# First stage of a graph kernel: its bulk loads issued by SyncE between the rounds instead of by ScalarE at the start

## The reference

```python
x0, x1 = _lin_irreps(x0, x1, W_up0, W_up1)          # of the layer-normed x, 1250 nodes x 512
h = edge_feats                                       # 40000 edges x 8
for W in (W_mlp1, W_mlp2, W_mlp3):
    h = SILU_2MOM * jax.nn.silu(h @ W / jnp.sqrt(jnp.float32(W.shape[0])))
tpw = h @ W_mlp4 / jnp.sqrt(jnp.float32(W_mlp4.shape[0]))
s0 = x0[sender]
s1 = x1[sender]
...
msg0 = jax.ops.segment_sum(m0, receiver, num_segments=num_nodes)
```

## Time and profile before

| | us |
|---|---|
| median of 3 runs | 2354.38 (2353.44 to 2356.39) |
| the profiled execution | 2353.07 |
| its span | 2351.4 |
| TensorE busy | 2003.0 (85%) |
| VectorE busy | 1513.0 (64%) |
| ScalarE busy | 1118.3 (48%) |
| mean traffic | 121 GB/s |

### The profile page before, as it was taken

How to read it: one execution, slowest core, us unless ns; L and a number is a source line. 1 busy time by engine, 2 the same in 40 slices (tenths; PEclk the granted TensorE clock), 3 DMA queues, 4 the chain that set the end, 5 groups by cost and what they waited for, 6 DMA issues and landing times. The chain is left out here.

```text
span 2351.4 us, 36494 instructions
## 1 busy us (share of the span) xinstructions
PE 2003.0 (85%) x11260; PEld 1288.4 (55%) x11261; DVE 1513.0 (64%) x2331; ACT 1118.3 (48%) x2278; POOL 748.9 (32%) x629
## 2 busy tenths in 40 slices
PE   5899999999997738999975497999999999980997
PEld 2444444444445727777732444777344777540997
DVE  1289999999995774333348865777763778428011
ACT  5777777777773404555510313666001676210332
POOL 4287777777770012444453000000000000000453
PEclk9989999999998957999988598999999999995998
DMA  5565555555551423788544313000012100221794
GB/s 160 168 170 157 154 155 154 153 154 152 155 155 53 95 85 129 268 261 265 174 129 132 96 43 115 22 22 1 18 43 81 64 22 1 104 100 46 221 277 94
DMA packets 200741, 285.12 MB, mean 121 GB/s; under 512 B 116698, under 2 KB 128677, under 8 KB 196543
## 3 DMA queue, kind: packets, MB, share of 16 engines
q0 software_dynamic: 98272, 142.08, 21.2%
q1 hardware_dynamic: 100158, 137.67, 19.0%
q10 hardware_dynamic: 2209, 4.07, 0.5%
HBM read 233.52 MB, written 49.84 MB: 121 GB/s over the span
## 5 line engine op out<-in xcount | busy, mean ns | idle before, releaser
L565 POOL DMA_INDIRECT p_s<-node_table,e_src_rows x320 | 454.5, 1420 | 147.4 <-issue 86.7
L2004 PE MATMUL g_psO<-g_h,g_ring 125*125 125x257 f32 x1600 | 372.4, 388 | 19.7 <-DVE g_ring L2136 10.3
L2004 PEld LDWEIGHTS g_psO<-g_h,g_ring 125*125 125x125 f32 x1600 | 296.6, 190 | 92.1 <-DVE g_stage L2130 26.6
L703 PE MATMUL p_psW<-e_w,p_hid 64*125 64x512 f32 x640 | 275.4, 654 | 50.2 <-ACT z L580 24.7
L622 DVE TENSOR_TENSOR g_b<-z,p_s 125x1536 f32<-125x1536 f32 x160 | 273.6, 1751 | 0.0
L711 PE MATMUL p_psM<-g_b 125*32 125x384 f32 x648 | 249.5, 533 | 11.0 <-DVE p_key L684 5.9
L580 ACT ACTIVATE z<-p_psW 125x512 f32<-125x512 f32 x320 | 187.2, 585 | 147.0 <-PE p_psW L703 139.0
L715 PE MATMUL p_psM<-g_b 125*32 125x256 f32 x648 | 218.8, 422 | 0.0
L714 PE MATMUL p_psM<-g_b 125*32 125x256 f32 x648 | 211.3, 410 | 0.0
L713 PE MATMUL p_psM<-g_b 125*32 125x256 f32 x648 | 193.8, 426 | 0.0
L585 ACT ACTIVATE p_of<-e_node_ids,z 125x314 bf16<-125x314 f16 x320 | 176.2, 551 | 6.8 <-PE p_psC L720 3.1
(11 more groups left out here) (357 smaller groups left out, 3775.2 us busy)
## 6 DMA issues: line engine op xcount, KB each, us to landing
p_ring<-in_L_ffn_weights SPq DMA_DIRECT2D x32, 1025.0 KB
slot_rows<-p_y POOLq DMA_DIRECT2D x70, 256.0 KB
p_w1s<-in_L_ffn_w SPq DMA_DIRECT2D x16, 1024.0 KB
g_a<-in_L_ffn_w SPq DMA_DIRECT2D x16, 1024.0 KB
hidden<-g_b SPq DMA_DIRECT2D x40, 250.0 KB, 3.2
p_hid<-hidden SPq DMA_DIRECT2D x160, 62.5 KB
g_rb<-receiver_rows SPq DMA_DIRECT2D x16, 610.4 KB
p_s<-node_table,e_src_rows POOLq DMA_INDIRECT x320
```

The lines of the kernel that those rows point to most:

```text
L565: pool.indirect_dma_start(s[:, g % 4, c, :, :].rearrange("p k u -> p (k u)"), None, node_table, bass.IndirectOffsetOnAxis(ap=src_rows[:, g ...
L703: nc.tensor.matmul(psW[c % 2][0:P, :], hid[part, b, c // 2, :], w4[part, :], start=True, stop=True)\
L2004: last = nc.tensor.matmul(psO[0:P, j, 0:HW], ring[:, i % RING, j * P:(j + 1) * P], h[:, s, hd, :], start=s == 0, stop=s == T - 1)
```

## The change

The 13 bulk loads are taken out of ScalarE's program and put into SyncE's, in four portions, each behind the stores of a round: two loads of x behind round 0, three behind round 1, dst and W_up behind round 2, the rest behind round 3. LEAD goes from 4 to 5, so the node tiles go with rounds 5 to 9 in place of 4 to 8, and all that is placed by LEAD (the square root, the table's way through DRAM, the scaling of w4) comes one round later.

```diff
-    LEAD = 4
+    LEAD = 5
...
+                rows = x.rearrange("(t p) d -> p t d", p=P)
+
+                def rows_in(k):
+                    sp.dma_start(xs[:, 2 * k:2 * k + 2, :], rows[:, 2 * k:2 * k + 2, :]).then_inc(x_in[k], 16)
+
                 for i in range(ITER):
                     if i + EB < ITER:
                         load(i + EB)
...
                             .then_inc(h3_out[b], 16)
+                    if i == 0:
+                        rows_in(0)
+                        rows_in(1)
+                    if i == 1:
+                        for k in range(2, T // 2):
+                            rows_in(k)
+                    if i == 2:
+                        sp.dma_start(dsts[:], dst.rearrange("(g e) -> g e", e=EG)).then_inc(dst_in, 16)
+                        sp.dma_start(wu[:, 0, :], w_up0).then_inc(up_in, 16)
+                        sp.dma_start(wu[:, 1, :], w_up1).then_inc(up_in, 16)
+                    if i == 3:
+                        sp.dma_start(tables.dst_rows[:].rearrange("p g c -> p (g c)"), dst_p).then_inc(all_in, 16)
+                        sp.dma_start(tables.src_rows[:].rearrange("p g c -> p (g c)"), src).then_inc(all_in, 16)
+                        sp.dma_start(tables.y[:].rearrange("p g c m -> p (g c m)"), ea4).then_inc(all_in, 16)
+                        for half in range(2):
+                            sp.dma_start(tables.w4[half * HID:(half + 1) * HID, :], w_mlp4).then_inc(all_in, 16)
...
-                rows = x.rearrange("(t p) d -> p t d", p=P)
-                for k in range(T // 2):
-                    act.dma_start(xs[:, 2 * k:2 * k + 2, :], rows[:, 2 * k:2 * k + 2, :]).then_inc(x_in[k], 16)
-                act.dma_start(dsts[:], dst.rearrange("(g e) -> g e", e=EG)).then_inc(dst_in, 16)
...
```

## The result

Median 2358.59 us (20 runs, 2350.54 to 2365.70) against 2353.39 for the kernel before (20 runs, 2344.94 to 2356.39): ratio 1.0024, 95% interval 1.0014 to 1.0034, some 5.6 us slower (3.3 to 8.0; the two medians themselves lie 5.2 apart). The forecast was 2355.6, +1.2 us, with a range of 2347.5 to 2361. The profiled execution took 2354.63 (span 2352.7); it is one of the quicker ones, so its 1.6 us over the profile of before understates the difference.

The account below looks back on a forecast made before the run. ScalarE was taken to bound the first stage, its Silus starting late behind 13 loads. Terms -13.5 + 2.5 + 9.3 + 2.3 + 0.6 gave +1.2 us, 2355.6 against 2354.38, range 2347.5 to 2361.

Parts of the forecast that it names:

- the 114 that was to count against the forecast: End of the first stage: the forecast counted as wrong if, despite the stall, it ended before 106 or after 114 us.
- the share: DMA share during the waits of rounds 2 and 3: expected at 0.33 from 22 to 31 and 34 to 47 us.
- Part 1: Stage start: with the loads off ScalarE's queue, the first Silu comes at 12.9, a gain of 13.5 us (12.9 to 14.3).
- Part 2: SyncE's queue: stores wait behind the loads, stalling the third Silus of round 2 by 2.5 and round 3 by 9.3 us.
- two premises: SyncE's queue: a load of 125 partitions uses about 5 of 16 DMA engines, and each engine works a queue in order.
- The rival in which the stores are not held: Rounds 2 and 3: no stall behind the loads, so -12.9 us, 2341.5; chance 0.12.
- Cold TensorE: Round 4: after standing from about 40 to 49, TensorE runs at the lower clock, cost 2.3 us (0 to 6.1).
- The rival in which the lower clock costs rounds 4 and 5 in full: Rounds 4 and 5: TensorE stays at the lower clock, +5 to +8 us, 2359.4 to 2362; chance 0.11.
- Part 3: Node tiles one round later: stage end costs 1.25, less 0.65 for a plain round, in all 0.6 us.
- All free: Rounds 4 to 9: the statistics of x and the table's detour, moved with the node tiles, were claimed to cost nothing.

Follow-up runs that it names:

- same_again: The changed kernel once more, no edit, for a second profile: 2350.75 us, ratio 1.0028 to the kernel before.
- before_again: The kernel before once more, no edit, for a second profile: 2345.31 us, ratio 1.0003.
- no_bases: The changed kernel without the store of bases, its load reading the first 80 words of dst instead: 2349.02 us, ratio 1.0019 to the kernel before.
- warm: The changed kernel with six extra matmuls into an unused bank behind round 3, while TensorE waits: 2350.30 us, ratio 1.0021 to the kernel before.
- warm_longer: The changed kernel with nine extra matmuls into an unused bank behind round 3: 2349.03 us, ratio 1.0019 to the kernel before.
- x_112_13: The changed kernel with each load of x cut in two, partitions 0 to 111 and 112 to 124: 2336.96 us, ratio 0.9968 to the kernel before.
- act_between: The changed kernel's portions in the same rounds, but issued by ScalarE on its own queue, LEAD 5: 2352.37 us, ratio 1.0035 to the kernel before.
- lead_only: The kernel before with LEAD = 5 alone: 2348.28 us, ratio 1.0007.
- pool_start: Against the kernel before, the 13 loads issued by GpSimd at the start, LEAD 4: 2338.50 us, ratio 0.9973.
- x_one_each: The changed kernel with one x load behind each of rounds 0 to 4, dst and W_up behind 3, rest behind 5: 2353.08 us, ratio 1.0037 to before.

## Why the prediction was right, and where it was off

The sum said +1.2, the runs +5.6 (3.3 to 8.0). The median lies in the range, but near its slow end, and the sum lies outside the interval; the change of 0.24% is just past the 0.2% that the forecast had called no change, with an interval on both sides of it. Two of the signs named beforehand also went another way. The next stage began at 118.64 in one of the two profiles, past the 114 that was to count against the forecast. And the share, meant to be 0.33 from 22 to 31 and from 34 to 47, was 0.66 to 0.90 from 22 to 28 and 0.51 to 1.05 from 40 to 46. The mechanism held; one step failed, and one agreement below is luck. In the table "changed" is the profile of after and that of same_again, "before" that of before and before_again:

| point, us | before | predicted | changed |
|---|---|---|---|
| first Silu | 26.39, 27.24 | 12.9 | 11.49, 11.57 |
| round 2's third Silus start | | 32.9 | 32.47, 32.72 |
| round 3's third Silus start | | 48.3 | 48.66, 48.93 |
| table load of the square root | 52.66, 53.63 | 59.4 | 59.94, 61.35 |
| next stage | 109.32, 110.40 | 110.5 | 112.78, 118.64 |
| table load to next stage | 56.66, 56.77 | 51.1 | 52.84, 57.29 |

- **Part 1** was low by 1.4 us: the edge tile, no longer beside the bulk, let TensorE start at 9.46 (12.38 before). It brought nothing: round 2's stall grew from 2.5 to about 4.0 (the wait of 3.43, and four Silus paced over 2.63 in place of 2.02), and its end is where it was predicted.
- **Part 2** gave both landings to about 0.6 us in these two profiles, and that of round 2 by luck. The stores of round 0 were issued at 17.28, not at 19.3, so by the prediction's own steps the first landing was due at 30.9 and came at 32.47. What took 1.6 us longer was the block on the five engines: after the stores, of the first two loads 43 rows moved from 21 to 23, where later 60 moved in each us, and the last of their 500 rows came just before 31. Two errors of opposite sign cancelled; why x started so slowly no run tells. In the three other profiles with the same start (no_bases, warm, warm_longer) the two Silus began at 33.20 to 33.75 and 49.44 to 50.76, up to 2.5 later than predicted. Of the two premises the five engines are shown by x_112_13, and the order within one queue by the packets after the change beside those of act_between. The rival in which the stores are not held is out. The rule of the Trainium skill that it was built on ("DMA: Bandwidth & Descriptors", Issuing engines are not separate DMA queues), by which the choice of the issuing engine saves only issue time, is not refuted by that: it speaks of which engine issues, and what cost 10.7 us here is the place in the queue. Taken as the worth of this change, though, it misses by that sum.
- **Cold TensorE** was priced at 2.3 with bounds 0 and 6.1; round 4 cost 2.3 in one profile and 3.4 in the other, and nothing extra in warm_longer. What I missed is that the clock falls behind the short stand of round 2 as well (0.50 in 34 to 38). In the changed kernel that hides in round 3's wait; in x_112_13 it was the largest cost left. The rival in which the lower clock costs rounds 4 and 5 in full is out, though its +5 to +8 is near the +5.6 that was measured: from the first Silu of the first tile round to that of the next it is 9.89 us after and 10.67 in same_again, against 9.83 and 9.93 in the two profiles of before, and 8.63 in a later tile round of each.
- **Part 3 is the step that failed**, its words "All free" above all. From the table load to the next stage it had 51.1. Without the store of `bases` the stretch takes 52.33 (62.74 to 115.07), so 1.2 of the error is sizes: 0.8 at the end, since from the last Silu to the next stage it took 5.6, not 4.8, and 0.4 in round 5 (10.23 from first Silu to first Silu, 9.83 before). With the store it took 52.84, 57.29, and 53.3 to 55.5 in x_112_13, act_between, warm, warm_longer and lead_only. All seven have a wait in round 7, of 0.7 to 2.6 us, and in two of them (same_again, lead_only) the clock falls behind it; in same_again round 8 then takes 11.27 us, in after 8.63. I had checked that the table's way through DRAM is in time for VectorE, and not what its stores do to their neighbours:

```profile
80.99 0.85 SPq L250 DMA_DIRECT2D steps<-p_tabi  x1
81.89 0.92 SPq L251 DMA_DIRECT2D bases<-p_ext  x1
```
```profile
hidden<-g_b SPq DMA_DIRECT2D x1, 250.0 KB, 8.8
...
steps<-p_tabi SPq DMA_DIRECT2D x1, 1.2 KB, 3.9
bases<-p_ext SPq DMA_DIRECT2D x1, 0.3 KB, 8.0
```

These are issues and landings (the last number, us from issue) of after: 0.3 KB, 80 single words, take 8.0 us to land, and the store of h3 issued just ahead of them 8.8, where one in a free queue takes 2.2 to 3.0. That store is issued at 80.50 and its tile is due to be overwritten at 88.60, 8.1 later. In the kernel before, where the pair goes behind round 5, no store takes more than 6.2 (6.5 in before_again), which is in time. There the words take 7.6 too, yet the store issued 0.5 us ahead of the pair lands after 3.2. So slow words alone don't hold up their neighbour.

**What stays open.** No run tells why the store ahead of the pair takes 8.8 to 10.6 us with LEAD 5 (5.0 without `bases`), and 3.2 to 3.8 with LEAD 4, where the waits for stores behind it are none, or 0.26 in pool_start. That no_bases is free of the wait is one profile. Also how the 5.6 us divide: the wait in round 7, the clock behind it and round 4's clock vary from one execution to the next, and the two profiles (+3.5 and, against before_again, +8.2) only bracket the median.

## What to carry to other kernels

Count the work of a DMA queue in the time of the engines that a shape uses, not in bytes: a load of 125 partitions took about five of sixteen engines, and cut into 112 and 13 partitions it took them all. The three kernels with that cut gained 7.5 to 10 us; of those without it the best, pool_start, gained 6.3, with an interval that overlaps theirs, and no other gained. Stores that set the pace of a loop should not stand behind such loads on their queue, and spreading the loads only moved the wait here, to whoever needs the last of them. When a block of work is moved by a round, check each small transfer in it for the room that its neighbours have, and count a stand of TensorE, even of less than 1 us, as the possible loss of its clock.

## What had not been expected of the hardware

- With about three loads of 125 x 2 rows in flight the issuer stood at the next one: three issues took 7.03 us on ScalarE and 6.48 us on SyncE; cut 112 + 13, ten issues took 5.08 in all.
- Loads and stores on one queue moved one behind the other on the five engines; on two queues they shared them, 17.3% and 15.8%.
- A store of 80 single words landed after 7.4 to 9.7 us in the profiles in which it stood behind plain stores. The 250 KB store ahead of it took 8.8 to 10.6 with LEAD 5 (12 and more in x_one_each, where loads stood in front), and 3.2 to 3.8 with LEAD 4.
- The length of a stand of TensorE didn't tell whether its clock would fall. It fell to the lower level behind stands of 0.35 us (x_112_13, round 3, granted clock 0.58 and 0.57 in two stretches of 4 us, a round of 9.2 in place of 6.1), 0.82 (same_again) and 1.26 (lead_only), and stayed at 1.00 behind 1.45 (warm_longer) and 1.90 (warm) in round 7.
- Loads issued by GpSimd delayed SyncE's small ones: the first edge tile landed at 19.4 in place of 12.4.
